# Attention with a gated dense branch on one core: put transfers on two queues, constants loaded in another order, three row maxima moved

## The reference

```
xn = layernorm(x)
q, k, v = xn @ wq + bq, xn @ wk + bk, xn @ wv + bv      # 32, 8, 8 heads of 16
q, k = rope(q), rope(k)
s = softmax(q k^T / 4) v                                  # no mask, 1024 x 1024 a head
z = xn @ W^T + b
m = sum_e p_e * (xn @ A_e) @ B_e
g = silu(z + min(0.5 |z| / (|m| + 1e-6), 1) * m)
out = x + s * g
```

## Time and profile before

| | us |
|---|---|
| median of 3 runs | 493.56 (493.24 to 493.92) |
| the profiled execution | 492.73 |
| its span, first to last instruction | 490.9 |
| TensorE busy | 459.1 (94%) |
| VectorE busy | 373.0 (76%) |
| ScalarE busy | 300.6 (61%) |
| GpSimd busy | 88.2 (18%) |
| mean granted TensorE clock | 0.989 of full |

### The profile page before, as it was taken

One profiled execution on the slowest core, in us unless ns is written; L12 is line 12 of the kernel. 1 busy time (PEld: TensorE's weight loads), 2 busy tenths in 40 slices (PEclk: granted clock), 3 DMA queues, 4 the chain that ended last, 5 costly groups with the idle time before them and its releaser, 6 DMA issues.

```text
span 490.9 us, 7226 instructions
## 1 busy us (share of the span) xinstructions
PE 459.1 (94%) x2469; PEld 187.7 (38%) x2469; DVE 373.0 (76%) x401; ACT 300.6 (61%) x593; POOL 88.2 (18%) x159
## 2 busy tenths in 40 slices
PE   8897999999999999999999999999999999999995
PEld 3573344443333333333333333333334333333331
DVE  6544788888988888898888888888888888334331
ACT  2210001236878787787878787787877787554474
POOL 8572223341010001001000100010010001013441
PEclk9999999997999999999999999999999999999999
DMA  8999944540000000000000000000000000020110
GB/s 268 281 125 126 121 66 67 76 66 1 1 1 1 3 1 3 1 1 1 1 3 0 3 0 3 1 1 3 0 3 0 3 0 3 2 76 0 39 29 29
DMA packets 13354, 17.32 MB, mean 35 GB/s; under 512 B 3088, under 2 KB 7440, under 8 KB 13328
## 3 DMA queue, kind: packets, MB, share of 16 engines
q1 hardware_dynamic: 11808, 15.84, 17.3%
q10 hardware_dynamic: 1520, 1.12, 0.8%
HBM read 6.72 MB, written 2.10 MB: 18 GB/s over the span
## 4 chain that ended last, share of the span: by engine, by line
PE 67%; ACT 16%; SPq 4%; DVE 4%; issue 4%; DMA 4%; POOL 0%; ACTq 0%; DVEq 0%
PE oT L859 26%; PE st L896 24%; ACT arena L545 16%; PE st L739 5%; PE sm L799 3%; PE sm L877 3%; SPq L290 2%; DMA kA<-arena 2%; PE sm L868 2%; DVE negmax L614 2%; DMA idb_sb<-in_identb 2%; PE oT L739 2%; SPq L258 1%; PE sm L880 1%; SPq L264 1%
## 5 line engine op out<-in xcount | busy, mean ns | idle before, releaser
L614 DVE TENSOR_REDUCE negmax<-sm 128x1 f32<-128x1024 f32 x256 | 303.4, 1220 | 50.0 <-PE sm L799 49.8
L545 ACT ACTIVATE arena<-st 128x512 f32<-128x512 f32 x512 | 266.1, 602 | 92.1 <-PE st L896 91.5
L896 PE MATMUL st<-qA,kA 50*128 50x512 f32 x512 | 192.6, 451 | 19.2 <-ACT arena L545 11.6
L799 PE MATMUL sm<-kA,qA 48*128 48x512 f32 x512 | 200.8, 466 | 3.8 <-DMA kA<-arena 3.4
L896 PEld LDWEIGHTS st<-qA,kA 50*128 50x128 f32 x512 | 85.4, 185 | 176.6 <-ACT arena L545 158.6
L859 PE MATMUL oT<-arena,vg 128*32 128x512 f32 x1024 | 138.1, 612 | 0.0
L799 PEld LDWEIGHTS sm<-kA,qA 48*128 48x128 f32 x512 | 84.7, 185 | 28.0 <-issue 12.6
L383 POOL TENSOR_TENSOR maxp<-negmax,consts 128x16 bf16<-128x16 f32 x16 | 3.4, 214 | 239.5 <-DVE negmax L614 239.5
L471 ACT ACTIVATE arena<-arena 128x512 fp32r<-128x512 f32 x10 | 6.3, 631 | 56.5 <-POOL arena L346 56.5
L859 PEld LDWEIGHTS oT<-arena,vg 128*32 128x32 f32 x1024 | 20.3, 108 | 31.4 <-ACT arena L545 24.7
L693 DVE TENSOR_TENSOR xT_sb<-sm,b_sb 128x512 f32<-128x512 f32 x4 | 2.8, 692 | 23.6 <-PE sm L880 23.6
(11 more groups left out here) (88 smaller groups left out, 248.5 us busy)
## 6 DMA issues: line engine op xcount, KB each, us to landing
qA<-arena SPq DMA_DIRECT2D x48, 128.0 KB, 5.1
x_sb<-in_x SPq DMA_DIRECT2D x8, 256.0 KB, 5.9
kA<-arena SPq DMA_DIRECT2D x12, 128.0 KB, 6.8
wT_sb<-in_wT SPq DMA_DIRECT2D x1, 1024.0 KB, 9.4
out<-x_sb SPq DMA_DIRECT2D x1, 896.0 KB, 4.0
out<-x_sb SPq DMA_DIRECT2D x4, 224.0 KB, 1.9
z_sb<-in_wq SPq DMA_DIRECT2D x1, 768.0 KB, 10.3
wkv<-in_wk ACTq DMA_DIRECT2D x1, 256.0 KB, 4.3
```

What stands on the lines that cost most here:

```text
L545: act.activation(probs[:, s % PB, h, :], st[:, (st_score(0, s, h) - late) % 3, :], ACT.Exp, scale=float(D) ** -0.5).then_inc(st_free, 1)
L614: dve.tensor_reduce(negmax[:, half, r:r + 1], sm[:, bank, :], AX.X, ALU.max, negate=True).then_inc(sm_free, 1)
L799: mm = pe.matmul(sm[:, bank, kh * HALF:(kh + 1) * HALF], qA[rows, half, g // 2, h, qt * P:(qt + 1) * P], kA[rows, g // 2, kh * HALF:(kh + ...
L896: pe.matmul(st[:, (st_score(0, s, h) - fewer) % 3, :], kA[rows, g // 2, kt * P:(kt + 1) * P], qA[rows, half, g // 2, h, :], start=True, st ...
```

## The change

- The odd halves of bias and tables, four loads, go from SyncE's queue to ScalarE's, behind its own four.
- idb (a bf16 identity) gets a semaphore of its own, `idb_in`. VectorE's first rotation waits for the four bias loads alone, no longer for idb as well.
- wT, B and b get a semaphore of their own, `late_in`. Together with bv and idb they are issued by SyncE behind its puts of the third half (n == 2). bv still counts on `wv_in`, and TensorE's wait for `wv_in` at 32 ahead of the values is unchanged.
- The puts of the first four halves (`ACT_STACKS = 4`) are issued by two queues: SyncE the even rows, ScalarE the odd ones, behind its cast of that half. From the fifth half on SyncE issues all six.
- In `MIXED` three maxima move from the last two entries (z2 from 3 to 2, z3 from 2 to 0) to the first (q10 from 0 to 3).

```diff
+ACT_STACKS = 4
-MIXED = [("q", (1, 0), 0), ("q", (1, 1), 3), ("u", 0, 4), ("q", (2, 0), 3), ("u", 1, 4), ("q", (2, 1), 3), ("z", 0, 3),
-         ("q", (3, 0), 2), ("z", 1, 3), ("q", (3, 1), 2), ("z", 2, 3), ("z", 3, 2)]
+MIXED = [("q", (1, 0), 3), ("q", (1, 1), 3), ("u", 0, 4), ("q", (2, 0), 3), ("u", 1, 4), ("q", (2, 1), 3), ("z", 0, 3),
+         ("q", (3, 0), 2), ("z", 1, 3), ("q", (3, 1), 2), ("z", 2, 2), ("z", 3, 0)]
...
+        def stack(queue, n, part, odd):
+
+            kind, i = halves[n]
+            for slot, of in enumerate(K_SLOTS if kind == "k" else Q_SLOTS):
+                if of == part:
+                    rows = slice(odd * ROWS + slot * D, odd * ROWS + (slot + 1) * D)
+                    to = kA[rows, :, i * HALF:(i + 1) * HALF] if kind == "k" else qA[rows, i[1], i[0], :, :]
+                    queue.dma_start(to.bitcast(F32), parts[odd * ROWS:(odd + 1) * ROWS, n % PART_BUFS, part, :]
+                                    ).then_inc(stacked[n], 16)
...
             sp.dma_start(wv_sb, wv.rearrange("(c p) n -> p c n", p=P)).then_inc(wv_in, 16)
-            load_tables(sp, 1)
             sp.dma_start(z_sb[:, :, P:E], wq_v[:, :, P:E]).then_inc(wq_in, 16)
             sp.dma_start(A_sb[:, :, :], A.rearrange("(c p) n -> p c n", p=P)).then_inc(ffn_in, 16)
             sp.dma_start(p_sb[:, :], p_sc).then_inc(ffn_in, 16)
-            sp.dma_start(idb_sb[:, :], identb).then_inc(small_in, 16)
-            sp.dma_start(bv_sb[:, :], bv.partition_broadcast(P)).then_inc(wv_in, 16)
-            sp.dma_start(wT_sb[:, :, :], wT.rearrange("(c p) n -> p c n", p=P)).then_inc(ffn_in, 16)
-            sp.dma_start(B_sb[:, :], B).then_inc(ffn_in, 16)
-            sp.dma_start(b_sb[:, :], b.partition_broadcast(P)).then_inc(ffn_in, 16)
+
+            def load_late():
+                sp.dma_start(bv_sb[:, :], bv.partition_broadcast(P)).then_inc(wv_in, 16)
+                sp.dma_start(wT_sb[:, :, :], wT.rearrange("(c p) n -> p c n", p=P)).then_inc(late_in, 16)
+                sp.dma_start(B_sb[:, :], B).then_inc(late_in, 16)
+                sp.dma_start(b_sb[:, :], b.partition_broadcast(P)).then_inc(late_in, 16)
+                sp.dma_start(idb_sb[:, :], identb).then_inc(idb_in, 16)
...
+                for part in range(PARTS):
+                    sp.wait_ge((part1, part2)[part], n + 1)
+                    stack(sp, n, part, 0)
+                    if n >= ACT_STACKS:
+                        stack(sp, n, part, 1)
+                if n == 2:
+                    load_late()
...
             load_tables(act, 0)
+            load_tables(act, 1)
...
+            act.wait_ge(ones_set, 1)
             for n in range(len(halves) - 2):
                 cast(n)
+                if n < ACT_STACKS:
+                    act.wait_ge(part1, n + 1)
+                    stack(act, n, 0, 1)
+                    act.wait_ge(part2, n + 1)
+                    stack(act, n, 1, 1)
```

More of the change, by code:

```diff
@@ L209, in build @@
         x_in = [sem(f"x_in{t}") for t in range(NT)]
-        wk_in, wq0_in, wq_in, wv_in, tab_in, ffn_in, small_in = (sem(n) for n in (
-            "wk_in", "wq0_in", "wq_in", "wv_in", "tab_in", "ffn_in", "small_in"))
-        id_in, ones_set = sem("id_in"), sem("ones_set")
+        wk_in, wq0_in, wq_in, wv_in, tab_in, ffn_in, late_in, small_in = (sem(n) for n in (
+            "wk_in", "wq0_in", "wq_in", "wv_in", "tab_in", "ffn_in", "late_in", "small_in"))
+        id_in, idb_in, ones_set = sem("id_in"), sem("idb_in"), sem("ones_set")
         zeros_set, wq_put = sem("zeros_set"), sem("wq_put")
@@ L478, in _ @@
                     e = PJ_AT["u", hh]
-                    act.wait_ge(ffn_in, 80)
+                    act.wait_ge(ffn_in, 32)
                     act.wait_ge(pj_full, e + 1)
@@ L597, in rope @@
                                          ALU.add, ALU.mult).then_inc(sin_mul, 1)
-            dve.wait_ge(small_in, 80)
+            dve.wait_ge(small_in, 64)
             dve.wait_ge(tab_in, 64)
@@ L635, in _ @@
                 if (kind, i) == ("z", 0):
-                    dve.wait_ge(ffn_in, 80)
+                    dve.wait_ge(late_in, 48)
                 for r in range(rows):
@@ L821, in _ @@
                 if (kind, i) == ("u", 0):
-                    pe.wait_ge(ffn_in, 80)
+                    pe.wait_ge(ffn_in, 32)
                 if kind == "u":
                     project("u", i, A_sb, slice(0, RANK), xT[:, i], rows)
+                if (kind, i) == ("z", 0):
+                    pe.wait_ge(late_in, 48)
                 if kind == "z":
@@ L832, in _ @@
                 if (kind, i) == ("z", 1):
-                    pe.wait_ge(small_in, 80)
+                    pe.wait_ge(idb_in, 16)
                     n = PJ_AT["max0", 0]
```

## The result

The changed kernel takes 503.93 us (median of 4 runs, 503.5 to 504.96) against 493.52 us for the kernel before; the ratio is 1.0213, with a 95% interval of 1.0196 to 1.0231. It is slower by 10.4 us. The forecast was 505.3. The span of its profiled execution is 501.7 us, 10.8 above the 490.9 of before.

A forecast was written before the change was run, and what follows sets the result against it. TensorE, busy for 94% of the span, was taken to bound the kernel. 14.8 + 1.8 - 5.1 + 0.3 = 11.8 us on 492.7 gave 504.5, with 0.8 for the median 505.3; 8-in-10 range 497 to 507.5.

The forecast's parts named there:

- values start later: Value projections wait for bv behind eighteen puts and start at 44.4 in place of 29.6: +14.8 us.
- values at low clock: Value projections after TensorE's idle of 16 us run at 1.2 GHz: +1.8 us, between 0 and 2.3.
- hole and its low clock go: Ahead of the first row maxima: the 3.44 us hole and 1.65 us of slow matmuls behind it go, -5.1 us.
- maxima at the front: First mixed projection takes three maxima from the last two and may lose a little: +0.3 us, between 0 and 0.6.
- first group's start: Start of the first group: no term in the sum; 2.3 us coming back appeared only in a rival.
- span: Whole profiled execution: the sum of the terms, +11.8 us on the span of 490.9.
- The low clock on return: TensorE back from its wait for bv runs the values at 1.2 GHz: +1.8 us, between 0 and 2.3.
- The rotation chain: VectorE's first rotation starts 2.9 us sooner; GpSimd's first sum moves to 20.8, the first put to 22.8, 1.4 us sooner.
- The maxima: Three maxima moved from the last two projections to the first: +0.3 us, between 0 and 0.6.
- The tail: First group's start, rival: a denser end keeps the clock up, 2.3 us come back; kernel faster, chance 0.05.
- The rival with overlapping queues: Puts on two queues: doubled rate, 0.52 us a put, gives 496.3; overlap or a leading queue, chance 0.24.
- The two rivals of the other sign: Tail's clock kept, bv before about 34, 492.4 (faster, 0.05); or bv at 32.6, gain and loss cancel, 493.6 (no change, 0.04).

The follow-up runs named there:

- e1: Kernel before with only bv's load moved behind the third half's puts: 506.52 us, ratio 1.0228 to the kernel before.
- e10: Changed kernel with bv, still late, on its own semaphore, so TensorE waits for wv alone: 496.07 us, ratio 1.007 to the kernel before.
- e9: Changed kernel plus 76 extra matmuls on zeros ahead of TensorE's wait for bv: 502.90 us, ratio 1.0191 to the kernel before.
- e4: Changed kernel with the maxima of the kernel before, bv still late: 503.85 us, ratio 1.019 to the kernel before.
- e6: Changed kernel with all puts on SyncE's queue (ACT_STACKS = 0): 504.82 us, ratio 1.021 to the kernel before.
- e7: Kernel before with only the three maxima moved to the first projection: 498.97 us, ratio 1.0114 to the kernel before.
- e2: Changed kernel with bv's load back ahead of the puts: 496.68 us, ratio 1.0063 to the kernel before.
- e3: Changed kernel with bv's load back ahead of the puts and the maxima of the kernel before: 492.73 us, ratio 0.996 to the kernel before.
- e5: Changed kernel plus 37 extra matmuls on zeros ahead of TensorE's wait for bv: 504.53 us, ratio 1.0206 to the kernel before.
- e8: Changed kernel with bv's load ahead of the puts and no maxima in the first two projections: 486.40 us, ratio 0.9832 to the kernel before.
- e11: Kernel before with only the maxima reordered, none in the first two projections: 489.24 us, ratio 0.9907 to the kernel before.

## Why the prediction was right, and where its terms were off

The mechanism was the one forecast: values behind bv, bv behind eighteen puts, a low clock on return, no hole ahead of the maxima. e1 and e10 show it by runs. The terms, against the profiled executions:

| term | forecast | measured | from |
|---|---|---|---|
| values start later | +14.8 | +15.05 | 44.65 against 29.60 |
| values at low clock | +1.8 | +1.78 | 9.09 against 7.31; e9: 7.41 with the clock kept |
| hole and its low clock go | -5.1 | -5.1 | 55.39 waits for nothing, 1.98 for four |
| maxima at the front | +0.3 | 0.0 | first group starts at 121.50 against 109.75, +11.75 in all; the terms above make 11.73 |
| first group's start | 0 | -0.97 | value products 6.57 us apart (first to third), before 7.54 |
| span | +11.8 | +10.8 | 501.7 against 490.9 |

Of the 1.4 us between 505.3 and 503.93, 1.0 is the span. The other 0.4 is what I put on top for the median: 0.8 us above the profiled execution, measured 0.43.

**The low clock on return** was met within 0.02 us, and that is luck. The 1.8 was a choice between 0 and 2.3, and the values behind the same wait took 9.53 us in e4, 9.20 in e6 and 10.20 in e1, which makes the term 1.9 to 2.9.

**The rotation chain** was half a microsecond later than worked out: wq came at 18.71, as assumed, but GpSimd's six copies took 2.63 us where they had taken 2.11. All of it is the first copy, 0.91 us in place of 0.40: it began at 18.71, 0.1 us behind VectorE's third rotation instruction (18.61 to 19.36), which before came at 21.35, behind the copies. In e9 wq came at 19.08, when that instruction was over, and the six took 2.11 again, with the next half's rotation beside them. The sum began at 21.30 (forecast 20.8) and the first put was issued at 23.33 (22.8). A slightly faster put (1.035 for 1.045 us) gave 0.2 of it back, so bv came 0.25 us later than forecast.

**The maxima** were mis-sized by 0.3 us, and e4 shows that they count for nothing here. Only e7 and e2 show their real price, 4 to 5.5 us, which appears as soon as bv is no longer what TensorE waits for. Of the change's own sum this was invisible.

**The tail** is where the missing microsecond is. I had priced the low clock at the first group's start as a rival, tied to the maxima that left the end. It did move, by 1 us of the 2.3:

```profile
127.72 1.93 PE L877 MATMUL oT<-arena,vg 128*32 128x512 f32 x8
131.44 1.06 PE L877 MATMUL oT<-arena,vg 128*32 128x512 f32 x8
134.29 1.06 PE L877 MATMUL oT<-arena,vg 128*32 128x512 f32 x8
```

But the cause I named for it doesn't fit the traces. The shorter stretch came with the old maxima (e1, e4) and with the new ones (the changed kernel, e7, e9), and the longer one with either too (before and e3; e2, e5, e6 and e10); e8 had the longer and e11 the shorter with one and the same table. What decides it stays open: no run changed it on purpose, each kernel has one trace, and the last section shows that the low stretches differ between executions of one kernel too. So the -0.97 may be no effect of the change at all.

**The rival with overlapping queues** fell with e6 and the changed kernel's own rows: 1.035 us a put with two queues, 1.07 or 1.045 (before) with one, not 0.52. The Trainium skill's page SBUF — State Buffer had both rules. Its measured 6% for two concurrent DMAs ("Can I just issue two DMAs to hit both halves?") is of the size of the 1 to 3% here; its port rule ("Door 1: The DMA port swizzle") did not turn into a doubled rate for puts that alternate between the two sets of partitions.

**The two rivals of the other sign** needed bv by 34, and bv was issued at 32.09; the 3.4 us of an empty engine alone would have been too late.

## What to carry to other kernels

When a load is moved back, look for the semaphore it counts on and list everything that waits for that count, not what reads the data: bv was read by GpSimd at 104 us in the kernel before, but its count stood ahead of TensorE's values at 29.6. A small transfer behind a backlog costs the backlog, and the backlog is read from the growth of issue-to-landing times, not from the issue times. And where an engine waits for a transfer, first look whether its own later work can be put ahead of the wait: twelve numbers in a table gave 0.9% alone (e11) and 1.7% together with the change's earlier start (e8, on another chip).

## What the runs showed of the hardware that I had not expected

A matmul on zeros in bf16 of 128 x 512 took 0.22 us at full clock (76 in 16.57 us), so a stretch of the length of bv's wait takes twice as many as I had counted. In e5 TensorE was busy for 8.15 us and idle for 8.47, and the clock was at half when work returned, just as after 16.74 us of idling. In e8 a wait of 1.56 us left it at full, and so did the 1.72 us ahead of the transposes in the earlier trace rows, while behind the 2.33 us there in e1 the eight transposes took 1.94 us in place of 1.06.

The clock did not fall and rise with the work. Behind the hole of the earlier trace rows it was still at full when TensorE took up work again at 45.51, fell at 46.8 and was back at 50.2. In e10 it fell at 41.0, within the hole, and stayed at half until 54.6, through 10.4 us of work. e2 has the same order on TensorE and a longer hole (8.44 us), yet its clock was back at 50.3. In e3 a hole of 4.21 us was followed by a low stretch from 44.4 to 54.6. Executions of one kernel differ as well: eight of e10's twelve took 495.2 to 497.4 us at a mean granted clock of 0.979 to 0.984, four, the profiled one among them, 499.9 to 500.3 at 0.969 to 0.973. I have no explanation for the length of a low stretch. A difference of a microsecond or two between two traces can be no more than that, and is to be shown over many executions before it is given a cause.
